# Head attention's scores on TensorE: products of four tokens with four, in 64x64 tiles, instead of eight with eight

## The reference, cut to what matters

```python
# layer 0, xn = layernorm(x); 16 heads of 64
qkv = xn @ w_qkv + b_qkv
qkv = qkv.reshape(B, L, 16, 3 * 64)
q, k, v = jnp.split(qkv, 3, axis=-1)
k = k + pos_enc[None, :, None, :]
attn = jnp.einsum('blhd,blgd->blhg', q, k) / sqrt(64)   # per token: 16 x 16
attn = softmax(attn, axis=-1)
out = jnp.einsum('blhg,blgd->blhd', attn, v)
return out.reshape(B, L, 1024) @ w_out + b_out
```

## Time and profile before

| What | us |
|---|---|
| Timed runs (median; lowest, highest) | 1117.93; 1117.87, 1118.39 |
| Profiled execution, span from first to last instruction | 1115.6 |
| Head attention's 16 turns: scores of turn 0 start, of turn 15 start | 20.74, 193.32 |
| TensorE busy in the whole span | 1100.7 |

### The profile page before, as it was taken

How to read it: one execution, slowest core, us unless ns; L and a number is a source line. 1 busy time by engine, 2 the same in 40 slices (tenths; PEclk the granted TensorE clock), 3 DMA queues, 4 the chain that set the end, 5 groups by cost and what they waited for, 6 DMA issues and landing times.

```text
span 1115.6 us, 21181 instructions
## 1 busy us (share of the span) xinstructions
PE 1100.7 (99%) x8399; PEld 706.2 (63%) x8399; DVE 846.0 (76%) x1246; ACT 591.8 (53%) x939; POOL 795.7 (71%) x524
## 2 busy tenths in 40 slices
PE   9999999999999999999999999999999999999998
PEld 7899889777755555455455455455455555457886
DVE  4868897666686878878878888888888888896554
ACT  4534334566666555555555455555555555554443
POOL 5778888754367889888888888898889898950000
PEclk9999999999999999999999999999999999999999
DMA  7322223300000002000000000000000000000000
GB/s 251 127 77 80 95 77 115 94 24 1 1 1 1 1 1 105 1 1 1 1 1 1 1 1 1 1 1 1 1 1 1 1 1 1 1 1 10 9 1 19
DMA packets 25601, 30.97 MB, mean 28 GB/s; under 512 B 2064, under 2 KB 21904, under 8 KB 24224
## 3 DMA queue, kind: packets, MB, share of 16 engines
q1 hardware_dynamic: 25184, 29.62, 7.9%
q10 hardware_dynamic: 320, 0.01, 0.0%
HBM read 20.19 MB, written 9.44 MB: 27 GB/s over the span
## 4 chain that ended last, share of the span: by engine, by line
PE 88%; DVE 7%; issue 2%; ACT 2%; POOL 2%; DVEq 0%; POOLq 0%; ACTq 0%
PE o_ps L1713 19%; PE mx_ps L1667 7%; PE st_ps L1697 5%; PE st_ps L1691 5%; PE st_ps L1694 5%; PE ha_banks L647 5%; PE bank L2126 3%; PE bank L2127 3%; PE bank L2128 3%; PE mx_ps L1600 3%; PE pj_ps L1619 2%; PE pj_ps L1611 2%; PE ha_banks L698 2%; PE ha_banks L667 2%; PE ha_banks L709 2%
## 5 line engine op out<-in xcount | busy, mean ns | idle before, releaser
L2040 POOL TENSOR_TENSOR acc<-acc,prob 128x1024 f32<-128x1024 f32 x192 | 468.6, 2440 | 61.9 <-ACT prob L1861 51.7
L1861 ACT ACTIVATE prob<-st_ps 128x1024 f32<-128x1024 f32 x256 | 248.5, 1023 | 206.4 <-PE st_ps L1697 206.3
L1713 PE MATMUL o_ps<-prob,v_cur 128*64 128x512 f32 x1024 | 245.7, 599 | 0.0
L1932 DVE TENSOR_REDUCE mx_part<-mx_ps 128x1 f32<-128x512 f32 x258 | 164.9, 667 | 72.0 <-PE mx_ps L1667 72.0
L1713 PEld LDWEIGHTS o_ps<-prob,v_cur 128*64 128x64 f32 x1024 | 68.1, 136 | 96.2 <-issue 77.5
L1935 DVE TENSOR_REDUCE mx_part<-mx_ps 128x2 f32<-128x1024 f32 x78 | 93.7, 1201 | 44.1 <-PE mx_ps L1667 44.1
L1951 DVE RECIPROCAL rden<-rden 128x128 f32<-128x128 f32 x128 | 120.6, 942 | 0.0
L1667 PEld LDWEIGHTS mx_ps<-k_hi,q_hi 64*128 64x128 f32 x414 | 46.6, 183 | 107.0 <-issue 94.6
L1667 PE MATMUL mx_ps<-k_hi,q_hi 64*128 64x512 f32 x414 | 111.7, 457 | 1.5 <-DVE mx_part L1935 0.8
L1697 PE MATMUL st_ps<-q_hi,d_lo 64*128 64x512 f32 x512 | 100.8, 390 | 0.0
L2040 POOL TENSOR_TENSOR acc<-prob 128x1024 f32<-128x1024 f32 x32 | 76.1, 2378 | 26.2 <-PE pj_ps L1596 18.9
(11 more groups left out here) (419 smaller groups left out, 2349.3 us busy)
## 6 DMA issues: line engine op xcount, KB each, us to landing
v_rows<-ha_v SPq DMA_DIRECT2D x8, 1024.0 KB, 3.9
ha_vt<-v_rows SPq DMA_DIRECT2D x16, 512.0 KB, 4.0
h_w<-in_h SPq DMA_DIRECT2D x2, 1024.0 KB, 8.1
w_raw<-in_w SPq DMA_DIRECT2D x8, 192.0 KB, 3.2
head_wkv<-in_wkv SPq DMA_DIRECT2D x2, 512.0 KB, 6.0
m_w<-in_m SPq DMA_DIRECT2D x3, 256.0 KB, 3.1
out<-fin SPq DMA_DIRECT2D x3, 256.0 KB, 2.3
sel_raw<-in_sel SPq DMA_DIRECT2D x1, 576.0 KB, 11.5
```

The lines of the kernel that those rows point to most:

```text
L1713: mm = pe.matmul(o_ps[rows(h), :], v_cur[:, m % 2, j, rows(h)], prob[:, (16 * m + slot) % RING, h, :], start=(j == 0), stop=(j == KT - 1), ...
L1861: act.activation(prob[:, n % RING, :, :], st_ps[:, slot % 2, :, :], ACT.Exp, scale=SCALE).then_inc(s_exp, 1)
L1932: dve.reduce_max(mx_part[:, h, i, keys:keys + 1], maxima_banks(q, n)[h], AX_X).then_inc(s_mxr, 1)
L2040: pool.tensor_tensor(total, old, new, ALU.add).then_inc(s_acc, 1)
```

## The change

Scores are multiplied for four tokens with four: per group of eight tokens and per sequence, two products of 64x64, the first four tokens' results in partitions 0 to 63 and the last four tokens' in 64 to 127. `q` is laid out in groups of four tokens, the mask and the masked scores shrink to half, the second half of each bank stays unused. The mask by heads is loaded in two pieces and made in two instructions. The turned probabilities come out in the order half, head, token of four, which `pt` and the wide products follow.

```diff
@@ sync, first loads
-        sp.dma_start(w.mask_h[:, :], a["mask"].rearrange("(t h) n -> h t n", h=HEADS)).then_inc(s_mask, 16)
+        for low in range(2):
+            of = slice(HD * low, HD * low + HD)
+            sp.dma_start(w.mask_h[of, :], a["mask"][of, :].rearrange("(t h) n -> h t n", h=HEADS)).then_inc(s_mask, 16)
@@ head_attention
+    FEW = G // 2
...
-    q, k = zip(*((room.sb(f"q{i}", [P, BLK // G, HEADS, G]), room.sb(f"k{i}", [P, HEADS, BLK])) for i in range(2)))
+    q, k = zip(*((room.sb(f"q{i}", [P, BLK // FEW, HEADS, FEW]), room.sb(f"k{i}", [P, HEADS, BLK])) for i in range(2)))
...
-    same = room.sb("same", [P, HEADS, G])
+    same = room.sb("same", [P, HEADS, FEW])
-    sm = [room.sb(f"sm{i}", [P, SEQS * GROUPS // 2, HEADS, G]) for i in range(2)]
+    sm = [room.sb(f"sm{i}", [P, SEQS, GROUPS // 2, HEADS * FEW]) for i in range(2)]
...
-    pt = room.sb("pt", [P, SEQS, HEADS, G])
+    pt = room.sb("pt", [P, SEQS, G // FEW, HEADS, FEW])
@@ tensor_scores
-            for seq in range(SEQS):
-                mm = pe.matmul(s_ps[half][:, seq, tile(g)], q[i // 2 % 2][rows(seq), of, :, :],
-                               k[i // 2 % 2][rows(seq), :, of * G:of * G + G], start=True, stop=True)
+            for low in range(G // FEW):
+                few = of * G + low * FEW
+                for seq in range(SEQS):
+                    mm = pe.matmul(s_ps[half][rows(low), seq, g * HD:g * HD + HD], q[i // 2 % 2][rows(seq), few // FEW, :, :],
+                                   k[i // 2 % 2][rows(seq), :, few:few + FEW], start=True, stop=True, skip_group_check=True)
@@ vector_same, vector_reduce, vector_masks
-        dve.tensor_tensor(sm[half][:, :, :, :], s_ps[half][:, :, :].rearrange("r s (g h t) -> r (s g) h t", g=GROUPS // 2, t=G),
-                          same[:, :, :].unsqueeze(1).to_broadcast([P, SEQS * GROUPS // 2, HEADS, G]), ALU.mult)\
+        scores = s_ps[half][:, :, 0:GROUPS // 2 * HD].rearrange("r s (g n) -> r s g n", n=HD)
+        own_token = same[:, :, :].rearrange("r h t -> r (h t)").unsqueeze(1).unsqueeze(1)
+        dve.tensor_tensor(sm[half][:, :, :, :], scores, own_token.to_broadcast([P, SEQS, GROUPS // 2, HD]), ALU.mult)\
...
-                       sm[half][:, :, :, :].rearrange("r (s g) h t -> r s g h t", s=SEQS), AX_X).then_inc(s_red, 1)
+                       sm[half][:, :, :, :].rearrange("r s g (h t) -> r s g h t", t=FEW), AX_X).then_inc(s_red, 1)
...
-        dve.wait_ge(f.s_mask, 32)
-        dve.tensor_scalar(same[:, :, :], w.mask_h[:, :].rearrange("r (t h) -> r h t", h=HEADS), 0.0, None, ALU.is_ge)
+        dve.wait_ge(f.s_mask, 16 * 3)
+        for low in range(G // FEW):
+            dve.tensor_scalar(same[rows(low), :, :], w.mask_h[rows(low), rows(low)].rearrange("r (t h) -> r h t", h=HEADS),
+                              0.0, None, ALU.is_ge)
@@ scalar_project, scalar_turned, gpsimd_wide
-            d = act.activation(q[b % 2][:, :, h, :], pj_ps[n % 2][:, j, :].rearrange("r (g t) -> r g t", t=G),
+            d = act.activation(q[b % 2][:, :, h, :], pj_ps[n % 2][:, j, :].rearrange("r (g t) -> r g t", t=FEW),
...
-        act.activation(pt[:, :, :, :].rearrange("r s h t -> r (s h t)"), p_ps, ACT.Copy).then_inc(s_ptc, 1)
+        act.activation(pt[:, :, :, :, :].rearrange("r s l h t -> r (s l h t)"), p_ps, ACT.Copy).then_inc(s_ptc, 1)
...
-            t = pt[:, seq, :, r * G // 2:r * G // 2 + G // 2].rearrange("r h t -> r t h")
+            t = pt[:, seq, r, :, :].rearrange("r h t -> r t h")
```

## The result

The changed kernel takes 1103.12 us (median of 4 runs, 1102.82 to 1104.86); the kernel before, on the same chip, 1118.16 (4 runs, 1117.87 to 1118.42). The ratio is 0.987, with an interval of 0.9856 to 0.9884: faster by 15.0 us, or 1.3%. The profiled execution took 1103.15 us with a span of 1100.9, so again some 2.3 us lie outside the span, which itself is 14.7 us shorter than before.

What follows compares the result with a forecast made beforehand. TensorE was taken to set the pace in head attention. 14.6 + 0.8 - 0.4 = 15.0 us took the span from 1115.6 to 1100.6; with 2.3 outside it, 1102.9 us (chance 0.54), range 1099.8 to 1114.5.

Steps and rivals of the forecast that it cites:

- Scores, 14.6 us: TensorE's head-attention scores: four array quarters at once, 2.06 to 1.15 us per turn, 0.91 gained in each of sixteen turns.
- rival B: TensorE scores: a floor on starts between 15 and 29 ns, whoever's tile; at 21, gain 8 us, 1109; chance 0.14.
- VectorE: Mask product and sum halve, 34 us in all off the path; 0.8 us back from TensorE's value-eviction wait.
- Small new waits, -0.4: TensorE: new waits, such as value evictions against a quicker TensorE, cost 0.4 us.
- GpSimd at zero: GpSimd costs nothing: VectorE's inverse comes some 1.8 us earlier after the scores' start, more than the 0.91 pulled in.
- rival C: GpSimd holds the turn: the key projection loses 0.91 in seven odd turns, 6.4 us back, 1109; chance 0.12.
- One sign: Expected in the profile after: GpSimd's wait for the inverse down, and no wait for GpSimd on TensorE.
- Masks, SyncE, ScalarE at zero: Extra mask load (0.59 us), second small mask instruction and ScalarE's query evictions in runs of four: all cost nothing.
- rival A: TensorE scores: only two quarters at once, 2.08 us for 2.06, leaving VectorE's 0.8; 1117; chance 0.11.
- rival D: TensorE scores: tiles split both ways do not overlap, 3.7 us for 2.06, +26 us, 1143; chance 0.09.

Runs made afterwards that it cites:

- experiment 1: Changed kernel with score products reordered, output halves one after the other, so neighbours differ only in the input half (two quarters at once): 1108.91 us.
- experiment 2: Changed kernel with score products reordered, four in a row in each quarter of the array before the next quarter: 1127.76 us.
- experiment 10: Changed kernel with score products reordered, input halves one after the other, so neighbours differ in the output half: 1108.85 us.
- experiment 3: Changed kernel with a further VectorE mask product and sum over three quarters of the values, ahead of each real one, into unread memory: 1109.98 us.
- experiment 4: Changed kernel with scores split further, two tokens with two in 64x32 tiles, 128 records a turn: 1120.03 us.
- experiment 8: experiment 4 with two projection units between the two halves of a turn's scores: 1114.97 us.
- experiment 5: Changed kernel with only the further VectorE mask product over three quarters of the values, sums left short: 1107.84 us.
- experiment 6: Changed kernel with only the further VectorE sum over three quarters of the values, mask products left short: 1105.40 us.
- experiment 7: Changed kernel with one more GpSimd addition of 256 values behind each subtraction, into a tile nobody reads: 1103.93 us.

## Why the prediction was right

The forecast was 1102.9 us; 1103.12 was measured. Point by point:

- **Scores, 14.6 us.** L698's pace for 32 records as the time of 64: 1.15 forecast, 1.16 measured, so 0.90 and not 0.91 a turn, 14.4. The premise, that pairing by rows and by columns each halve the time and so quarter it together, is shown by experiments 1, 2 and 10: take one pairing away and the group grows to 1.56, take both and it is 2.69, and the whole kernel follows. In the changed kernel the starts lie in rounds of four.
- **The floor on starts (rival B).** The rows hold ten starts in 122 ns. The burst's 21 ns of the earlier trace rows was what that line needed, and no floor. The Trainium skill's rule (TensorE: Matmul & The Clock Gate, section "Wait — 56ns, not 53.3ns?"), that starts are never closer than some 25 ns, does not hold across tiles here.
- **VectorE.** Forecast 0.68 and 0.67 us, measured 0.684 and 0.676. What it returns directly was put at 0.8; the wait for the value eviction fell by 1.0.
- **Small new waits, -0.4.** All idle time together fell by 0.3 us, where 0.8 - 0.4 was forecast; with 1.0 returned the new waits come to 0.7. In reading the rows the prediction took the 0.26 us at 152.01 for a stop of TensorE and its loads; it is the loads' alone, and the products stood still for some 0.1. No term of the sum hangs on it.
- **GpSimd at zero (rival C).** Right, for the reason given: the inverse comes earlier after the scores' start, in most turns by 1.2 to 1.5 us where 1.8 were forecast, and still by more than the 0.9 of the scores. One sign failed: TensorE was to have no wait for GpSimd, and it has one, of 0.5 us. The sum understates what hangs on the cover. VectorE's part stands there with 0.8 us, but had its work stayed as long as before, 6.9 would have been lost (experiment 3), and more of that at the value eviction than on rival C's path. Less VectorE time is cover for the scores' gain and not a gain beside it; the two together make 15.0, and neither order of adding them gives each its own share.
- **Masks, SyncE, ScalarE at zero.** The copy of the value bias starts at 17.15 us without a wait, and both small instructions for the mask run ahead of the first value eviction, in VectorE's timeline of the changed kernel:

```profile
20.52 0.42 DVE L797 TENSOR_SCALAR ha_same<-ha_head_mask_h 64x64 f32<-64x64 f32 x2
...
21.17 0.69 DVE L776 TENSOR_TENSOR ha_v<-ha_banks,head_bv 128x512 f32<-128x512 f32 x1
21.77 1.28 DVE L783 TENSOR_TENSOR ha_sm<-ha_banks,ha_same 128x512 f32<-128x512 f32 x2
```

- **Rivals A and D.** Both spoke of how tiles overlap; both are ruled out for this order of products only. As chances they were taken for properties of the chip, while in these runs the loop order decides: at 2.69 us a turn the same tiles are a loss of 9.3 us against the kernel before. The prediction named the order of the quarters and did not price another one.

The sum was 15.0 and the spans say 14.7: the scores term was 0.2 too high and the idle term 0.1. That the medians lie 0.2 us from the forecast is closer than the terms are, and luck to that extent.

## What to carry to other kernels

When small products use separate parts of TensorE's array, issue them so that neighbours in the order lie in different parts, in rows and in columns: here that order alone was worth 1.16 against 1.56 and 2.69 us for the same 64 records. Splitting pays until the number of instructions takes its place; one step further (128 records in 1.4 us) gave back all and more, since TensorE then ran out of instructions. And when a change shortens two engines, ask what the faster one would meet if the other had stayed: 6.9 of these 15.0 us needed VectorE's part as cover.

## What was not expected of the hardware

- **Starts in different quarters** lie a few ns apart (four within 22 ns) and 13.6 to 15 ns on average in 64x64 tiles, some 9 ns in 64x32 tiles (experiment 4).
- **A change of quarter hides 0.17 us**, three passes of 58 ns: the next quarter starts while three records ahead of it in the order are still to start (experiments 1, 2, 10).
- **TensorE can run out of instructions.** With 128 records of products and as many of weight loads in 1.4 us it stood idle for up to 1.8 us at a time with no releaser, 9.6 us in all, every time at a count of 256 instructions and until 1.3 to 1.5 us after a 16,384-byte packet of the instruction queue had landed; 2.6 us when the bursts are spread (experiments 4, 8).
- **A short stretch at the lower clock.** In experiments 2, 4 and 8 the granted clock fell to about half, the 1.2 GHz level, for some 3.4 us, once, early in the stage. In experiment 2 (the window, columns as above):

```profile
42.30:45.70 3.40, 3.40 (x38) 3.09 (x34) 1.38 (x2) 0.71 (x2) 3.03 (x4) 0.51 0.00 0
```

TensorE was busy without a break before it: products with one moving column (L219, 1.84 us from 39.13) and then scores one quarter at a time, whose group took 3.52 us for 2.69, and the product behind it 0.79 for 0.50. Such a stretch costs about 1.7 us. The changed kernel has the same L219 products at 36.14 and its clock stays at 1.00 in the profiled execution; in the run of 1104.86 us its mean was 0.998, which would fit one such stretch. The kernel before seems to have it too: of its eleven runs beside experiments 5 to 8, four have a mean clock of 0.998 and take 1120.06 to 1120.31 us, the other seven 1117.53 to 1118.63. What sets it off was not tried.
